# Quantising a layer's weights and placing the type slots at the start of layer 0 instead of in the setup before it

## The reference

```python
# layer 0, part 1: an adapter and a layer norm; its weights are chosen by the sequence's language id
h = relu(hidden @ W1[lang] + b1[lang]);  x = hidden + h @ W2[lang] + b2[lang]
normed = (x - mean) * rsqrt(var + 1e-05);  x = normed * gamma[lang] + beta[lang]
# layer 0, part 2: a gated feed-forward with weights quantised to -1, 0, 1
def _weight_quant(w):
    scale = 1.0 / clip(mean(abs(w)), 1e-05)
    return clip(round(w * scale), -1.0, 1.0) / scale
gate = silu(_bitlinear(x, w_gate)); up = _bitlinear(x, w_up)
x = x_in + _bitlinear(gate * up, w_down)        # activations rounded to 8 bits, row by row
# layer 1 begins with experts that are chosen by a type label of each sequence (5 types)
wi_sel = wi[type_label]; wo_sel = wo[type_label]
```

## Time and profile before

| what | value |
|---|---|
| median of 3 runs | 670.63 us (666.62 to 671.85) |
| the profiled execution's own time | 668.36 us |
| its span, first to last instruction | 666.2 us |
| granted TensorE clock, mean | 0.952 of full speed |
| busy: PE, DVE, ACT, POOL | 83%, 61%, 57%, 46% |
| setup ends, layer 0 begins | 21.6 us |
| first reciprocal root of POOL (block 0) | 40.0 us |
| busy share of the DMA engines, 25 to 70 us | nearly 1 |

### The profile page before, as it was taken

How to read it: one execution, slowest core, us unless ns; L and a number is a source line. 1 busy time by engine, 2 the same in 40 slices (tenths; PEclk the granted TensorE clock), 3 DMA queues, 4 the chain that set the end, 5 groups by cost and what they waited for, 6 DMA issues and landing times. The chain is left out here.

```text
span 666.2 us, 18696 instructions
## 1 busy us (share of the span) xinstructions
PE 554.1 (83%) x5740; PEld 462.7 (69%) x5749; DVE 407.2 (61%) x1450; ACT 382.7 (57%) x804; POOL 304.0 (46%) x316
## 2 busy tenths in 40 slices
PE   1478999866699995988999989998889689999950
PEld 1233555433699994867888878887778689999950
DVE  6325899896433331235668767788585756666636
ACT  0225776777456642346455655664777578888820
POOL 1246477774200002744137664456376664555430
PEclk9998999989699997999899999998899899999985
DMA  8999701111622210102055211023222122222229
GB/s 272 332 401 408 306 33 36 40 41 67 196 69 67 70 37 16 48 21 50 18 161 141 100 46 46 28 56 84 53 63 63 57 78 73 74 68 73 71 67 339
DMA packets 76313, 71.10 MB, mean 107 GB/s; under 512 B 26857, under 2 KB 63537, under 8 KB 75841
## 3 DMA queue, kind: packets, MB, share of 16 engines
q1 hardware_dynamic: 60976, 34.10, 18.1%
q10 hardware_dynamic: 8816, 22.64, 8.7%
q0 software_dynamic: 6432, 13.25, 6.2%
HBM read 30.31 MB, written 39.66 MB: 105 GB/s over the span
## 5 line engine op out<-in xcount | busy, mean ns | idle before, releaser
L1347 POOL DMA_INDIRECT y_dram<-u_hh,v_to x72 | 69.3, 962 | 65.3 <-DVE u_hh L2389 56.5
L1337 POOL DMA_INDIRECT rows_dram<-u_row,u_slots x64 | 62.8, 982 | 46.2 <-DVE u_slots L2268 26.5
L1487 PE MATMUL u_py<-cwo,u_hh 128*128 128x128 f32 x512 | 68.3, 281 | 0.8 <-ACT u_hh L1856 0.7
L1487 PEld LDWEIGHTS u_py<-cwo,u_hh 128*128 128x128 f32 x512 | 63.3, 193 | 5.4 <-issue 2.1
L1649 PE MATMUL u_py<-w,v_h 128*128 x384 | 54.2, 286 | 5.8 <-ACT v_h L1936 2.4
L1649 PEld LDWEIGHTS u_py<-w,v_h 128*128 128x128 f32 x384 | 48.3, 197 | 8.7 <-issue 8.6
L1630 PE MATMUL u_pz<-v_xT,v_held 128*128 128x128 f32 x384 | 53.0, 284 | 0.5 <-DVE v_h L2369 0.4
L1856 ACT ACTIVATE u_hh<-u_pz 128x512 f32<-128x512 f32 x64 | 38.0, 596 | 26.7 <-PE u_pz L1478 23.6
L1929 ACT ACTIVATE v_held<-w 128x512 f32 x72 | 45.6, 633 | 13.3 <-PE u_pz L1630 5.0
L1630 PEld LDWEIGHTS u_pz<-v_xT,v_held 128*128 128x128 f32 x384 | 48.8, 200 | 1.8 <-issue 1.4
L1936 ACT ACTIVATE v_h<-u_pz,p_bT 128x128 f32<-128x128 f32 x124 | 36.9, 369 | 11.0 <-PE u_pz L1630 8.9
(11 more groups left out here) (362 smaller groups left out, 1507.4 us busy)
## 6 DMA issues: line engine op xcount, KB each, us to landing
rows_dram<-zero ACTq DMA_DIRECT2D x1, 17160.0 KB, 57.7
v_x<-rows_dram SPq DMA_DIRECT2D x72, 65.0 KB
w<-in_mw SPq DMA_DIRECT2D x2, 2048.0 KB
cwt<-in_cw SPq DMA_DIRECT2D x1, 2560.0 KB, 15.3
xs_dram<-zero SPq DMA_DIRECT2D x1, 2304.0 KB, 16.2
e_xs<-xs_dram SPq DMA_DIRECT2D x36, 64.0 KB
eo_dram<-e_y SPq DMA_DIRECT2D x36, 64.0 KB
x_dram<-x SPq DMA_DIRECT2D x8, 256.0 KB, 2.0
```

What stands on the lines that cost most here:

```text
L1337: pool.indirect_dma_start(rows_dram, bass.IndirectOffsetOnAxis(ap=slots[:, q, k, u:u + 1], axis=0), row[:, q, k, u, :], None).then_inc(sen ...
L1347: pool.indirect_dma_start(y_dram, bass.IndirectOffsetOnAxis(ap=vto[t % XR][:], axis=0), vy[:, t % XR, :], None).then_inc(v_sent[t % XR], 16)
L1487: last = nc.tensor.matmul(py[:, u * D:(u + 1) * D], hh[:, e % HR, u * P:(u + 1) * P], cwo[:, m * KF + k], start=(k == 0 and u == 0), stop= ...
```

## The change

The sum of the absolute weights, the small product, the scaling and rounding and the type slots leave `setup`. They become the first work of DVE in layer 0. The product becomes PE's work there, ahead of the first block's hidden layer, and writes the PSUM tile `pu`. The tiles that both functions need are now made outside of them, and the setup copies the ranks out of PSUM (`rank`). The wait for the cleared rest of `hid` (`hid_padded`) moves from PE's start to the second product, and the wait for `magic` from ACT's start to the first place that uses it. PE waits for the rounded weights (`ffw_made`) before the first product that reads them. ACT runs one small activation (`warm`) at its start. The transfers, their queues, their order and POOL's list are unchanged.

```diff
@@ setup, sync
-                    sp.dma_start(ffw[:, n, :], a[name]).then_inc(ld_f, 16)
+                    sp.dma_start(ffw[:, n, :], a[name]).then_inc(ffw_loaded, 16)
@@ setup, vector
-                link(nc.vector.tensor_tensor(offs[:], endt[:], padf[:], ALU.subtract))
...
-                link(nc.vector.tensor_copy(type_of_tile[0:1, :], totile[0:1, :]))
+                link(nc.vector.tensor_copy(rank[:], ps3[:, 0:TYPES]))
...
-                dve.wait_ge(ld_f, 16 * 3)
-                nc.vector.tensor_reduce(tot[:], ffw[:], AX, ALU.add, apply_absolute_value=True).then_inc(sums, 1)
-
-                dve.wait_ge(means, 1)
...
-                    link(nc.vector.tensor_scalar(q, rnd[:, n, :], MAGIC, None, ALU.subtract))
                 dve.wait_ge(gbd, 1)
@@ setup, tensor
-                pe.wait_ge(sums, 1)
-                nc.tensor.matmul(ps[:, 0:3], ones[:], tot[:], start=True, stop=True).then_inc(means, 1)
@@ layer_zero, tensor
+                def prepared(i):
+                    if i != FIRST + 1:
+                        return
+                    pe.wait_ge(sums, 1)
+                    nc.tensor.matmul(pu[:, 0:3], ones[:], tot[:], start=True, stop=True).then_inc(means, 1)
...
                 def second(b):
+                    pe.wait_ge(hid_padded, 1)
...
                 def up(p, n):
+                    if s == 0:
+                        pe.wait_ge(ffw_made, 3)
...
                 pe.wait_ge(w_loaded, 16 * 4)
-                pe.wait_ge(hid_padded, 1)
                 for i in range(FIRST, LAST + 1):
+                    prepared(i)
@@ layer_zero, scalar
                 def quantise(p):
+                    act.wait_ge(magic_made, 1)
...
-                act.wait_ge(magic_made, 1)
+                act.activation(warm[:], zero[:, 0:1], ACT.Copy)
@@ layer_zero, vector
+                nc.vector.memset(magic[:], MAGIC).then_inc(magic_made, 1)
...
+                dve.wait_ge(ffw_loaded, 16 * 3)
+                nc.vector.tensor_reduce(tot[:], ffw[:], AX, ALU.add, apply_absolute_value=True).then_inc(sums, 1)
                 nc.vector.memset(hid[KT[-1][1]:P, :, NK - 1, :], 0.0).then_inc(hid_padded, 1)
-                nc.vector.memset(magic[:], MAGIC).then_inc(magic_made, 1)
+                dve.wait_ge(means, 1)
+                link(nc.vector.tensor_scalar(msc[:], pu[:, 0:3], 1.0 / (D * INNER), 1e-5, ALU.mult, ALU.max))
...
+                    nc.vector.tensor_scalar(q, rnd[:, n, :], MAGIC, None, ALU.subtract).then_inc(ffw_made, 1)
+                link(nc.vector.tensor_tensor(offs[:], endt[:], padf[:], ALU.subtract))
...
+                link(nc.vector.tensor_copy(type_of_tile[0:1, :], totile[0:1, :]))
```

More of the change, by code:

```diff
@@ L172, in adaln_ffn_moe_kernel @@
                 zero = sb("zero", [P, ZW], stack=layer0)
+                consts = sb("s_consts", [P, 3 * P + HG + 1 + TYPES + S + TT], stack=layer0)
+                ffw = sb("s_ffw", [P, 3, INNER], stack=layer0)
+                t1h, padf, endt, rank = (sb("s_" + n, [P, TYPES], stack=layer0) for n in ("t1h", "padf", "endt", "rank"))
                 x_loaded = [sem(f"x_loaded{q}") for q in range(NB)]
                 w_loaded, rows_cleared = sem("w_loaded"), sem("rows_cleared")
+                ffw_loaded = sem("ffw_loaded")
                 setup(nc, a, sb, pb, sem, x1, ident, tri, ones, hmask, low_part, type_slot, type_of_tile, xs_dram,
-                      w1, w2, bias1, tab, lang1h, gb, wgq, wuq, wdq, wsc, KT, zero, x_loaded, w_loaded, rows_cleared)
-                layer_zero(nc, a, sb, pb, sem, x1, ident, w1, w2, bias1, tab, lang1h, gb, KT, wgq, wuq, wdq, wsc,
-                           type_slot, xs_dram, x1_dram, rows_dram, zero, cwt, cws, cwo, b1, b2, ln2, prep, x_loaded, w_loaded, rows_cleared)
+                      w1, w2, bias1, tab, lang1h, gb, consts, ffw, t1h, padf, endt, rank, KT, zero, x_loaded, w_loaded, rows_cleared, ffw_loaded)
+                layer_zero(nc, a, sb, pb, sem, x1, ident, w1, w2, bias1, tab, lang1h, gb, KT, wgq, wuq, wdq, wsc, ones, tri, consts, ffw, t1h, padf, endt, rank, type_of_tile,
+                           type_slot, xs_dram, x1_dram, rows_dram, zero, cwt, cws, cwo, b1, b2, ln2, prep, x_loaded, w_loaded, rows_cleared,
+                           ffw_loaded)
             typed_experts(nc, sb, pb, sem, ident, ones, tri, hmask, low_part, type_slot, type_of_tile, x1_dram, x1t, xs_dram, eo_dram,
@@ L258, in setup @@
         ld_ty = sem("ld_ty", st)
[L259 to L262, removed]
+        ld_t, ld_c = (sem(n, st) for n in ("ld_t", "ld_c"))
+        cleared, diag, ranks, ty1h, tabs, step, gbd = (sem("s_" + n, st) for n in ("cleared", "diag", "ranks", "ty1h", "tabs", "step", "gbd"))
         C_I, C_T, C_1, C_H, C_M, C_P, C_S, C_J = np.cumsum([0, P, P, P, HG, 1, TYPES, S]).tolist()
@@ L385, in _, with layer_zero @@
                 nc.tensor.matmul(ps4[:, 0:2 * D], lang1h[:], tab[:, 0:2, :], start=True, stop=True).then_inc(gbd, 1)
-                pe.wait_ge(sums, 1)
-                nc.tensor.matmul(ps[:, 0:3], ones[:], tot[:], start=True, stop=True).then_inc(means, 1)
-def layer_zero(nc, a, sb, pb, sem, x1, ident, w1, w2, bias1, tab, lang1h, gb, KT, wgq, wuq, wdq, wsc,
-               type_slot, xs_dram, x1_dram, rows_dram, zero, cwt, cws, cwo, b1, b2, ln2, prep, x_loaded, w_loaded, rows_cleared):
+def layer_zero(nc, a, sb, pb, sem, x1, ident, w1, w2, bias1, tab, lang1h, gb, KT, wgq, wuq, wdq, wsc, ones, tri, consts, ffw, t1h, padf, endt, rank, type_of_tile,
+               type_slot, xs_dram, x1_dram, rows_dram, zero, cwt, cws, cwo, b1, b2, ln2, prep, x_loaded, w_loaded, rows_cleared,
+               ffw_loaded):
     NK = len(KT)
@@ L398, in layer_zero @@
         slots_cleared = sem("slots_cleared", st)
+        sums, means, step = (sem("q_" + n, st) for n in ("sums", "means", "step"))
+        warm = sb("l_warm", [P, 1], stack=st)
+        ffw_made = sem("ffw_made", st)
+        C_S, C_J = np.cumsum([3 * P + HG + 1 + TYPES, S]).tolist()
+        tot = sb("s_tot", [P, 3], stack=st)
+        msc = sb("s_msc", [P, 3], stack=st)
+        inv = sb("s_inv", [P, 3], stack=st)
+        rnd = sb("s_rnd", [P, 3, INNER], stack=st)
+        offs = sb("s_offs", [P, TYPES], stack=st)
+        slot = sb("s_slot", [P, TYPES], stack=st)
+        slotw = sb("s_slotw", [P, TYPES], stack=st)
+        slot1 = sb("s_slot1", [P, 1], stack=st)
+        row1 = sb("s_row1", [P, 1], stack=st)
+        tslot = sb("s_tslot", [P, S], stack=st)
+        past = sb("s_past", [1, TYPES - 1, TT], stack=st)
+        totile = sb("s_totile", [1, TT], stack=st)
         xT = sb("l_xT", [P, 2, W], stack=st)
@@ L707, in outer, with link @@
                     last.then_inc(x1_made, 1)
[L709 to L710 removed]
+                nc.vector.memset(magic[:], MAGIC).then_inc(magic_made, 1)
+                done = [0]
+                def link(ins):
+                    done[0] += 1
+                    ins.then_inc(step, 1)
+                    dve.wait_ge(step, done[0])
+                dve.wait_ge(ffw_loaded, 16 * 3)
@@ new lines, in _ @@
+                for n in range(3):
+                    link(nc.vector.tensor_scalar(rnd[:, n, :], ffw[:, n, :], inv[:, n:n + 1], MAGIC, ALU.mult, ALU.add))
+                link(nc.vector.tensor_scalar(rnd[:], rnd[:], MAGIC - 1.0, MAGIC + 1.0, ALU.max, ALU.min))
+                for n, q in enumerate((wgq[:], wuq[:], wdq[:].rearrange("p k d -> p (k d)"))):
+                    nc.vector.tensor_scalar(q, rnd[:, n, :], MAGIC, None, ALU.subtract).then_inc(ffw_made, 1)
+                link(nc.vector.tensor_tensor(offs[:], endt[:], padf[:], ALU.subtract))
@@ new lines, in _ @@
+                link(nc.vector.tensor_tensor(slot[:], offs[:], rank[:], ALU.add))
+                link(nc.vector.tensor_tensor(slotw[:], slot[:], t1h[:], ALU.mult))
+                link(nc.vector.tensor_reduce(slot1[:], slotw[:], AX, ALU.add))
+                link(nc.vector.tensor_scalar(row1[:], slot1[:], float(S), None, ALU.mult))
+                link(nc.vector.tensor_scalar(tslot[:], consts[:, C_S:C_J], row1[:, 0:1], None, ALU.add))
+                nc.vector.tensor_copy(type_slot[:], tslot[:])
```

42 lines of the change are left out of this document (7 added, 35 removed).

## The result

The changed kernel took 682.63 us in the median of 4 runs (678.28 to 688.50), against 668.62 us of the kernel before (four runs by now, 663.07 to 671.85). The ratio is 1.0207, with an interval of 1.0147 to 1.0267: about 2% slower. One of the four ran slow at a lower clock (688.50 us at 0.916, the others at 0.925 to 0.940), and ratios leave such runs out. The forecast had the direction and the mechanism right and the size too large: 693 us, so 22.4 more than the median of that time, where 14.0 more were measured. The profiled execution took 684.88 us, its span is 683.2 against 666.2 us, 17.0 more.

The account below looks back on a forecast made before the run. The prediction took one chain headed by the setup's end as the bound, with POOL then waiting for starved `xs_dram`. 21.4 + 2 = +23.4 us on 668.36 gives 691.8, by the median 694.0; it said 693, range 681 to 705.

Parts of the forecast that it names:

- Setup and gain: Setup to block 0: work leaving the setup starts layer 0 at 13.2 us and brings ACT's copy 9.9 us earlier.
- The collision: DMA queues at layer 0's start: `rows_dram` starves `xs_dram` packet by packet, so POOL's block 0 root comes 21.4 us later.
- Rivals 1 and 2: DMA queues: 1, sharing by bytes, 658 to 661 us, chance 0.12; 2, uneven turns, about 677 or 726, 0.03 together.
- Rival 3: Whole kernel: another engine holds the barrier, or gain and loss cancel, 666 to 673 us; chance 0.04.
- The lag: Queue q10: 3.3 us from issue of `rows_dram` to its first packets, so the slow stretch begins at 16.5 us.
- 6.8 us per us: Clearing of `xs_dram`: each us of lag is 42.5 packets per engine at 5.42 per us, less the 1 us.
- the slowest engine: DMA landing of `xs_dram`: the engine with 206 packets left when `rows_dram` starts decides, ending at 54.5 us.
- The mean engine: DMA landing of `xs_dram`: alternative with a mean of 174 packets left, ending at 48.5 us.
- the forecast's root: POOL's root of block 0: after the clearing, `raw` and the two splits, at 61.4 us; before it was 40.01.
- The clock: Term of +2 us in the sum, beside the 21.4 us by which block 0's root comes later.
- Sum: Whole time: 21.4 + 2 = +23.4 us on 668.36 gives 691.8; by the median 694.0; forecast 693.

Follow-up runs that it names:

- e1: Changed kernel, but ACT issues the clearing of `rows_dram` in its step i = -2, about 23 us instead of 13.2; median 755.13 us against 764.66.
- e11: Changed kernel with ACT issuing the clearing of `rows_dram` later, in its step i = -2, run on one chip over five rounds; ratio 0.9862, 757.21 us.
- e2: Changed kernel with `xs_dram` cleared in 768 pieces of 3072 bytes instead of 4608 of 512; ratio 0.9847.
- e4: Changed kernel, same transfers, but POOL waits for `xs_dram` only ahead of its first scatter and splits `raw` later; ratio 0.9868.
- e8: Kernel before, no work moved, with only the clearing of `rows_dram` issued later, in ACT's step i = -2; ratio 0.9995.
- e3: Kernel before, no work moved, with only the clearing of `rows_dram` issued early, in the setup; ratio 1.0187.
- e5: Changed kernel with `rows_dram` cleared in twice as many pieces of half the size (2080 bytes); one execution, 768.1 us beside 765.97.
- e10: Changed kernel again, unchanged, on one chip over five rounds; ratio 1.0131, 776.37 against 767.05 us.
- e12: Changed kernel with 46 extra products on PE in its hole, ahead of the first turn of rounded rows; 685.87 us, a single execution.

## Why the prediction held, step by step

**Setup and gain.** Layer 0's start was forecast at 13.2 us (13.19), ACT's copy at 15.4 (15.27), the first residual at 27.8 (27.62), a gain of 9.9. Only kernels whose POOL waits for no late transfer can show it at the root: 10.7 us in e1, 10.4 in e11, 10.1 in e2 and 10.5 in e4. Up to about 1 us of that is the pace of PE's products in block 0, which moved the root of e8 by as much with nothing gained.

**The collision.** Packet by packet, 87 per us against `rows_dram`: measured 443 / 5 = 89. e2, e3, e4 and e5 each change one link (size of one transfer, size of the other, time of the issue, POOL's wait) and each moved the root in the direction that the forecast's arithmetic gives, e2, e4 and e5 to within 1 us and e3 by half of what was expected. The start of the slow stretch in e3 was put some 0.6 us too early, which accounts for about half of that miss; the rest is open. That the collision makes the loss is shown. Rivals 1 and 2 fall with the equal counts from 17.5 us on, and with e2 and e5. Rival 3 falls with the time.

**The lag**, 3.3 us from issue to first packet, was the soft number, and it was 3.7 (issue 13.19, two packets before 17.0). By 6.8 us per us this takes 2.7 off. The rest of the 4.0 by which `xs_dram` beat its forecast (50.5 for 54.5) is small: from 16.9 us the slowest engine has 4.45 x 42.5 = 189 packets, and at 16 x 5 / 443 = 0.181 us they end at 51.1. The mean engine would have ended near 45, so to take the slowest was right. (The terms of the forecast's root add up to 61.3, not 61.4.) The lag to the first packet hardly differs between runs: 3.6 to 3.7 us in the changed kernel, e3, e4 and e10. What differs is when all engines share: the counts become equal near 17.5 us in the changed kernel and near 17.7 in e10, whose `xs_dram` landed 2.4 us sooner and whose root came 2.6 us earlier. So the loss moves by 2 to 3 us between executions of the same code, and why is open.

**The clock**, forecast at +2 us, is the term that was furthest off for its size. The 2 us were the author's estimate, and no run shows them: block 0 has slow products too (2.08 us a pair, later 1.02), but over them the granted clock was 1.00 (26.0 to 28.1 us in the kernel before). What the runs showed in its place is a low clock after the hole that cost 0.9 us at block 2 and nothing by block 3. The granted clock of the changed kernel after the hole, 67.5 to 77.5 us (PE, PEld, DVE, ACT, POOL busy, PEclk, DMA share, GB/s):

```profile
67.50:77.50 10.00, 9.84 (x25) 4.08 (x27) 2.58 (x12) 5.01 (x8) 6.69 (x7) 0.75 0.79 271
```

From 67.3 to 72.5 us the granted clock was 0.50 and its pairs took 1.92 and 1.97 us; from 72.5 to 77.5 it was 0.99, and the next pair, at 77.87, took 1.02. That delayed block 2's root by 0.9 us (24.09 from block 0's, before 23.21). In e10 the clock was 0.50 from 64.7 to 66 us, 0.67 to 69 and 1.00 from there on, and the distance is 23.22: no delay. And block 3 took it back: its root comes 13.47 us after block 2's, where the kernel before needed 15.18, since it had a slow stretch of its own there, with no hole ahead of it (granted clock 0.50 from 63.2 to 66 us and 0.62 from 67.9 to 69.7, where its L474 took 1.70 us; the changed kernel had 1.00 from 81.6 to 95.06, and its L458 at 85.29 took 1.07). Over the other kernels of the table blocks 0 to 3 take 36.7 to 38.3 us, before 38.4. So the honest size of this term is 0 to 1, inside that spread. What the forecast had no term for is that PE's pace differs between executions elsewhere in layer 0: 1.0 us in block 0 (e8, at a granted clock of 1.00 as before) and, at most, the 3.8 us in the drain (0.99 before, 0.59 changed).

**Sum.** 21.4 + 2 was forecast; 17.5 at the root and -0.8 up to block 7 were measured, and drain and later stages cancel to 0.3. On the span that is 17.0 for 23.4: 3.9 us of the miss are the collision (lag and rounding), 2.8 the term for the clock, with 0.3 back. The cancelling is luck, since the 3.76 us of the drain stand against a short one of before, and the 3.46 us behind it are within what such traces differ by (e12's rest takes 494.9 us, the changed kernel's 492.4, before 495.8). The size held only just: 682.63 lies 1.6 us above the lower end of 681 to 705, and e10's ratio on 668.62 us would give 677.4, below it.

## What to carry to other kernels

A wait that costs nothing may do so by a hair: the row to look at is when the awaited transfer lands against when the waiter arrives (21.55 and 21.60 us here). Before starting a stage earlier, ask which transfers start earlier with it and share a DMA engine with one that is still in flight. Two busy queues moved packet for packet in these traces (354 and 347 before, 443 and 443 changed, 90 and 90 in e2, 750 and 747 in e5), so the clearing in small pieces beside the one in large pieces was slowed by the time of the pair over that of its own packet (0.181 to 0.0235 us here, 7.7 times). Give it larger pieces, issue the large one later, or put the wait in front of the first instruction that needs it.

## What the runs showed that was not expected

The kernels took 741 to 795 us in the jobs of e1 to e11, the one before 759 to 775, and 663.0 (before) and 685.87 us (e12, both single executions) in the last, on the same chip as e5 to e8. Up to the end of the typed experts (272 us) the changed kernel and e10, which is the same code, are alike. The 93 us are lost in layer 1: 51 up to the end of L1508's products, 42 behind them. Part of it is what PE waited for ahead of the attention's scores (L1551, us, times), in the changed kernel and in e10:

```profile
  issue: 2.8, 8
```
```profile
  issue: 47.1, 85
```

PE waits there for nothing that the profile shows. The view adds up weight loads and products, which overlap in part (busy 78% and 64% of e10's span); the products alone waited 16.7 us in e10, 35 times, and not at all in the changed kernel. So this is a part of the 93 us, and the cause stays open.
